# Cross attention scores from one tile per head, with the key's high and low part stacked on the partitions

## The chip, the cores and the metric

The kernel runs on one core of one Trainium2 chip. The metric is the device time of that core in microseconds. A profile is one execution of the program, recorded by the hardware. TensorE (PE) does matmuls, and its weight loads are shown apart as PEld; VectorE is called DVE, ScalarE ACT, GpSimd POOL, and SyncE (SP) issues the DMAs. The engines run their own instruction streams and wait for each other by semaphores.

## The reference

The program is a perceiver block with three stages: a cross attention, a second attention, and a mixture of experts. The change is in the first, and in its inner part:

```
q = x @ Wq                        # 8 x 128 queries, after a layernorm; 16 heads of 64
k, v = split(context @ Wkv)       # 8 x 2048 keys
sim = einsum('bhid,bhjd->bhij', q, k) * 64 ** -0.5
sim = where(mask, sim, -big)
sim = clip(sim, -5, 5)
attn = softmax(sim)
out = einsum('bhij,bhjd->bhid', attn, v)
```

Matmuls run on operands rounded to a format with a short mantissa (`F32R`). To keep float32 accuracy, the kernel splits an operand into a high part (the rounded value) and a low part (the rounded rest), and adds three products: low by high, high by low, and high by high.

## The kernel before

`stage_cross` works in slots, 64 for each of 8 batches (`SL`), so 512 in all. A slot handles 128 keys (`kt`) and four heads (`GRP`, numbered by `GL` within a half `hf` of the 16 heads). Eight slots (`BS`) share one block of 512 keys: the first four slots take the heads of `GL` 0, the other four those of `GL` 1. Each engine's body writes its order out by hand, slot by slot; the middle batches are one loop on every engine but TensorE.

TensorE in a slot s (L621 to L649):
- waits that the projection of slot s - 2 is evacuated (`p_free`) and that the scores of slot s - 2 were clipped;
- scores: for each of two pairs of heads three matmuls of 256 columns (`K_lo` by `Q_hi`, `K_hi` by `Q_lo`, `K_hi` by `Q_hi`), summed in PSUM. A pair's key is 128 partitions, 64 for each head; its query is stored with zeros, so that the left 128 columns have one head and the right 128 the other. `ps_s` has two banks, one for each of two slots in turn;
- values of slot s - 2 (`LAG`): four matmuls of 256 columns with the exponentials' high and low part side by side;
- one unit of the projection of keys or values for a later block: twelve matmuls of 512 columns into `ps_p`. The order of the units over eight slots is K, K, V, V, K, K, V, V (`IN_SLOT`), the last four for the next block. At slot 4 of 8, TensorE first waits for all four pieces of the next context block's low part (`clo_done`). The last four slots of the last batch have no projection.

ACT in slot s: the high part of the projection unit of slot s - 1 (`evac_hi`, L455), the exponential twice (L489 rounded into `E2`, L493 in full into `E`), and in slots 4 to 7 of 8 the high part of a piece of context (`C_hi`, L499). DVE: the low part of the unit (`evac_lo`, L515), the clip of `ps_s` with the mask's bound as a column (L557), and `exp_lo` of slot s - 1 (L565), the low part of the exponentials. POOL: `sums` (L427), which adds up the exponentials, and `C_lo` (L435) in slots 4 to 7 of 8.

Some slots after the last of each group of heads (four groups a batch, 32 in all) come the group's closing steps, placed by `after(s, by)`: a high and a low part of the sums, four ACT copies of 64 partitions out of `ps_o` (L477, L478), two DVE additions of 64 partitions (L529), the totals on TensorE (L609), a reciprocal (L534), a product (L541) and the store.

Lines named elsewhere: L204 and L190 are a normalization on DVE and a low part on POOL in the stage ahead; L853 and L1289 are scalings on DVE in later stages.

## Time and profile before

| | |
|---|---|
| time, median of 3 runs | 3588.77 us (3583.67 to 3590.61) |
| the profiled execution | 3591.36 us |
| its span, first to last instruction | 3589.5 us |
| PE busy | 3316.7 us (92%) |
| PEld busy | 2847.9 us (79%) |
| DVE busy | 1851.6 us (52%) |
| ACT busy | 1485.4 us (41%) |
| POOL busy | 1631.7 us (45%) |

Busy shares are means over the span. In a timeline row the first number is the start in microseconds from the span's start, the second the duration; in brackets stands how long the engine was idle before it and what ended that. A matmul's duration includes its way through the array, so that a stream of them is paced by the distance of their starts.

### The profile page before, as it was taken

What the parts mean: (1) busy time and instruction counts of PE and PEld (TensorE: products, weight loads), DVE (VectorE), ACT (ScalarE), POOL (GpSimd) and SP (SyncE); (2) the same over time, 40 slices, a digit from 0 to 9 for tenths busy, and PEclk for the clock granted to TensorE, in tenths of its full rate; (3) what the DMA queues carried; (4) which work ended last, traced back from release to release, by engine and by line L of the source; (5) the groups of instructions that cost most, each with busy time, mean ns of one, the idle gap of its engine ahead of it and who ended that gap; (6) DMA issues with size and microseconds to landing.
All of it is one profiled execution on the core that took longest, in us unless ns stands there. A gap on an engine that the chain in (4) does not pass through costs nothing. (4 is left out here: it accounts for less than half of the span.)

```text
span 3589.5 us, 52832 instructions
## 1 busy us (share of the span) xinstructions
PE 3316.7 (92%) x19140; PEld 2847.9 (79%) x19140; DVE 1851.6 (52%) x3010; ACT 1485.4 (41%) x2749; POOL 1631.7 (45%) x1122
## 2 busy tenths in 40 slices
PE   5999999999999999999999988899999586799995
PEld 4888888888888888888888876777777465578995
DVE  4454555555455555555545557566566537432213
ACT  3455555555555555555555541244344214221000
POOL 4354555555455555545545543143144035146663
PEclk9999999999999999999999989899999798899998
DMA  5211111111111011111111004100000300123220
GB/s 194 76 33 36 45 45 44 35 35 46 36 45 46 24 45 46 43 38 45 33 36 45 27 15 139 55 1 26 3 1 1 108 16 1 49 74 118 83 83 24
DMA packets 116510, 170.33 MB, mean 47 GB/s; under 512 B 12288, under 2 KB 89472, under 8 KB 107520
## 3 DMA queue, kind: packets, MB, share of 16 engines
q1 hardware_dynamic: 113408, 158.23, 14.0%
q0 software_dynamic: 2816, 8.46, 0.7%
q8 instruction: 159, 2.61, 0.3%
q14 instruction: 127, 1.04, 0.1%
HBM read 143.52 MB, written 23.13 MB: 46 GB/s over the span
## 5 line engine op out<-in xcount | busy, mean ns | idle before, releaser
L427 POOL TENSOR_TENSOR es<-es,e 128x512 f32<-128x512 f32 x480 | 622.7, 1297 | 966.7 <-ACT e L493 966.5
L489 ACT ACTIVATE e_hl<-sc 128x512 fp32r<-128x512 f32 x512 | 325.2, 635 | 739.1 <-DVE sc L557 738.8
L585 PE MATMUL ps_p<-c_hi,wkv_lo 128*128 128x512 f32 x1024 | 402.4, 393 | 4.5 <-PEq L115 4.5
L515 DVE TENSOR_TENSOR k_lo<-ps_p,k_hi 128x512 fp32r<-128x512 f32 x256 | 175.9, 687 | 438.9 <-ACT k_hi L455 438.9
L585 PE MATMUL ps_p<-c_lo,wkv_hi 128*128 128x512 f32 x1024 | 401.9, 393 | 0.0
L585 PE MATMUL ps_p<-wkv_lo,c_hi 128*128 128x512 f32 x1024 | 401.6, 392 | 0.0
L585 PE MATMUL ps_p<-wkv_hi,c_lo 128*128 128x512 f32 x1024 | 401.5, 392 | 0.0
L585 PE MATMUL ps_p<-c_hi,wkv_hi 128*128 128x512 f32 x1024 | 398.8, 389 | 0.0
L515 DVE TENSOR_TENSOR v_hl<-ps_p,v_hl 128x512 fp32r<-128x512 f32 x256 | 177.2, 692 | 428.8 <-ACT v_hl L455 427.9
L585 PE MATMUL ps_p<-wkv_hi,c_hi 128*128 128x512 f32 x1024 | 398.3, 389 | 0.0
L557 DVE TENSOR_SCALAR sc<-ps_s,topi 128x512 f32<-128x512 f32 x512 | 380.0, 742 | 0.3 <-PE ps_s L635 0.2
L565 DVE TENSOR_TENSOR e_hl<-e,e_hl 128x512 fp32r<-128x512 f32 x512 | 353.6, 691 | 0.6 <-ACT e L493 0.6
L596 PE MATMUL ps_o<-e_hl,v_hl 128*128 128x256 f32 x2048 | 330.8, 284 | 1.2 <-DVE e_hl L565 1.1
L435 POOL TENSOR_TENSOR c_lo<-raw,c_hi 128x512 fp32r<-128x512 f32 x248 | 322.2, 1299 | 0.0
L493 ACT ACTIVATE e<-sc 128x512 f32<-128x512 f32 x512 | 315.7, 617 | 0.0
L635 PE MATMUL ps_s<-q_hi,k_hi 128*128 128x256 f32 x1024 | 289.7, 283 | 0.0
L635 PE MATMUL ps_s<-q_lo,k_hi 128*128 128x256 f32 x1024 | 289.6, 283 | 0.0
L635 PE MATMUL ps_s<-q_hi,k_lo 128*128 128x256 f32 x1024 | 287.3, 281 | 0.2 <-DVE v_hl L515 0.2
L596 PEld LDWEIGHTS ps_o<-e_hl,v_hl 128*128 128x128 f32 x2048 | 283.3, 192 | 2.7 <-DVE e_hl L565 2.4
L1024 POOL TENSOR_TENSOR a_s<-a_s,a_mx 128x1536 f32<-128x1536 f32 x32 | 88.1, 2753 | 347.7 <-DVE a_mx L1107 347.7
L585 PEld LDWEIGHTS ps_p<-c_hi,wkv_hi 128*128 128x128 f32 x1024 | 192.6, 188 | 42.1
L585 PEld LDWEIGHTS ps_p<-wkv_hi,c_hi 128*128 128x128 f32 x1024 | 192.4, 188 | 42.0
(399 smaller groups left out, 7136.4 us busy)
## 6 DMA issues: line engine op xcount, KB each, us to landing
raw<-in_ctx_t SPq DMA_DIRECT2D x64, 1024.0 KB, 4.9
dense_raw<-in_L_ffn_W_experts SPq DMA_DIRECT2D x64, 256.0 KB, 3.0
raw<-in_L_xattn_Wkv SPq DMA_DIRECT2D x4, 1024.0 KB, 5.0
q_hi_scratch<-qa_qh SPq DMA_DIRECT2D x16, 256.0 KB, 2.5
q_lo_scratch<-qa_ql SPq DMA_DIRECT2D x16, 256.0 KB, 3.4
q_hi<-q_hi_scratch SPq DMA_DIRECT2D x32, 128.0 KB, 5.1
q_lo<-q_lo_scratch SPq DMA_DIRECT2D x32, 128.0 KB, 4.7
o_t_scratch<-o_sb SPq DMA_DIRECT2D x32, 128.0 KB, 2.3
```

Source lines behind the costliest of these rows:

```text
L427: g.tensor_tensor(ES[:, GL], ES[:, GL], e, ALU.add).then_inc(summed, 1)
L435: g.tensor_tensor(C_lo[:, n % 2, k, :], RAW[:, n % 2, k, :], C_hi[:, n % 2, k, :].bitcast(F32), ALU.subtract).then_inc(clo_done, 1)
L489: a.activation(E2[:, s % 2, :, 0, :], sc, ACT.Exp, scale=DH ** -0.5).then_inc(exp_hi, 1)
L493: a.activation(E[:, s % 2], SC[:, s % 2], ACT.Exp, scale=DH ** -0.5).then_inc(expd, 1)
L515: v.tensor_tensor(kv_slice(False, kind, n), ps_view(u, kind), kv_slice(True, kind, n).bitcast(F32), ALU.subtract).then_inc(p_free, 1)
L557: v.tensor_scalar(SC[:, s % 2], ps_s[:, s % 2], topi[:, kt16:kt16 + 1], -RAW_CLIP, ALU.min, ALU.max).then_inc(clipped, 1)
L565: v.tensor_tensor(E2[:, s % 2, :, 1, :], E[:, s % 2].rearrange("p (j q) -> p j q", j=GRP), E2[:, s % 2, :, 0, :].bitcast(F32), ALU.subtrac ...
L585: mm = t.matmul(ps_p[:, par % 2, :], lhs, rhs, start=m == 0, stop=m == 3 * KC - 1)
L596: mm = t.matmul(ps_o[:, 2 * GL + j // 2, (j % 2) * 256:(j % 2 + 1) * 256], V2[:, kt, GRP * GL + j, :], E2[:, s % 2, j].rearrange("p e q -> ...
L635: mm = t.matmul(ps_s[:, s % 2, pr * 256:(pr + 1) * 256], k_[:, c, kt * P:(kt + 1) * P], q_[:, hf, c, :], start=n == 0, stop=n == 2)
L1024: g_.tensor_tensor(S[:, k % 3], S[:, k % 3], each(mx[:, k % 2]), ALU.subtract).then_inc(s_shifted, 1)
```

## The change

- Scores. The key's high and low part of one head now lie on top of each other, 64 partitions each, in `K2`; the query's high and low part, each repeated on both halves of the partitions, lie side by side in `Q2`. One matmul of 256 columns for a head gives (high + low key) by high query in the left 128 columns, and by low query in the right ones. A slot has four such matmuls. They fill both banks of `ps_s`, so the next slot's scores wait until both halves are read.
- Halves. ACT copies the right halves to `RIGHT`; DVE adds them to the left ones into `SC` (`halves_added`) and clips `SC` in place, now in SBUF.
- Evacuation of a key unit takes two instructions of 64 partitions each on ACT and on DVE. On ACT it now comes behind `RIGHT`, on DVE between the addition and the clip.
- ACT's exponentials of a slot move behind the evacuation of the next slot; `exp_lo` moves from DVE to POOL, ahead of `sums`, and `C_lo` from POOL to DVE, in slots 2, 3, 6 and 7 of 8, behind the clip. `C_lo` of slots 2 and 3 is the last that TensorE waits for at slot 4.
- Values follow three slots behind (`LAG` 3); the group steps come one slot later each.
- The zeroing of Q goes, the queries' DMAs move twice the bytes.

```diff
-LAG = 2
+LAG = 3
...
-        def has_split(s, last):
-            return s % BS >= KT and not (last and s // BS + 2 >= SLB)
+        def split_at(s):
+
+            return (s // BS, s % BS - 6) if s % BS >= 6 else (s // BS - 1, s % BS)
+
+        def has_split(s, first, last):
+            return s % KT >= 2 and not (last and split_at(s)[0] + 2 >= SLB) and not (first and split_at(s)[0] < 0)
...
-                for dst, src in ((Q_hi, q_hi_d), (Q_lo, q_lo_d)):
-                    for hh in range(2):
-                        sp.dma_start(dst[hh * DH:(hh + 1) * DH, hf, :, hh * P:(hh + 1) * P].bitcast(F32),
...
+                for e, src in enumerate((q_hi_d, q_lo_d)):
+                    for r in range(2):
+                        sp.dma_start(Q2[r * DH:(r + 1) * DH, hf, :, e * P:(e + 1) * P].bitcast(F32),
...
-            for Q in (Q_hi, Q_lo):
-                g.memset(Q[:].bitcast(F32), 0.0).then_inc(zeroed, 1)
...
+            def exp_lo(i, s):
+
+                g.wait_ge(expd, i * SL + s + 1)
+                g.tensor_tensor(E2[:, s % 2, :, 1, :], E[:, s % 2].rearrange("p (j q) -> p j q", j=GRP),
+                                E2[:, s % 2, :, 0, :].bitcast(F32), ALU.subtract).then_inc(e_lo, 1)
+
             def body(i, first, last):
                 for s in range(SL):
-                    S = i * SL + s
-                    sums(i, s, first)
-                    if has_split(s, last):
-                        n, k = s // BS, s % BS - KT
-                        g.wait_ge(chi_done, KC * (i * SLB + n) + k + 1)
-                        g.tensor_tensor(C_lo[:, n % 2, k, :], RAW[:, n % 2, k, :], C_hi[:, n % 2, k, :].bitcast(F32),
-                                        ALU.subtract).then_inc(clo_done, 1)
+                    if s or not first:
+                        exp_lo(i, s - 1)
+                        sums(i, s - 1, first)
                     group_steps(i, s, first)
...
+        def evacuated(kind, n, u):
+
             out = ps_p[:, u % 2, :]
-            return out if kind == K else out.rearrange("p (h d) -> p h d", d=DH)
+            if kind == V:
+                return [(V2[:, n, :, 0:DH], V2[:, n, :, DH:], out.rearrange("p (h d) -> p h d", d=DH))]
+            return [(K2[0:DH, n, hh, :], K2[DH:, n, hh, :], out[hh * DH:(hh + 1) * DH]) for hh in range(2)]
...
+                    a.wait_ge(scored, S + 1)
+                    a.copy(RIGHT[:], ps_s[:].rearrange("p b (j e q) -> p (b j) e q", j=2, e=2)[:, :, 1, :]).then_inc(right_out, 1)
                     if s and has_kv(s - 1, last) or s == 0 and not first:
-                        evac_hi(unit_at(i, s - 1), unit_at(0, s - 1), *unit_of((s - 1) % SL)[:2])
...
+                        evac_hi(unit_at(i, s - 1), unit_at(0, s - 1), kind, n)
+                    if s or not first:
+                        exps(i, s - 1, first)
...
+                    v.wait_ge(right_out, S + 1)
+                    if not (first and s < 2):
+                        v.wait_ge(expd, S - 1)
+                    v.tensor_tensor(SC[:, s % 2].rearrange("p (j q) -> p j q", j=GRP), ps_s[:].rearrange("p b (j e q) -> p (b j) e q", j=2, e=2)[:, :, 0, :],
+                                    RIGHT[:], ALU.add).then_inc(halves_added, 1)
                     if s and has_kv(s - 1, last) or s == 0 and not first:
                         evac_lo(unit_at(i, s - 1), unit_at(0, s - 1), *unit_of((s - 1) % SL)[:2])
...
-                    v.tensor_scalar(SC[:, s % 2], ps_s[:, s % 2], topi[:, kt16:kt16 + 1], -RAW_CLIP, ALU.min, ALU.max).then_inc(clipped, 1)
-                    if s or not first:
-                        exp_lo(i, s - 1)
+                    v.wait_ge(halves_added, S + 1)
+                    v.tensor_scalar(SC[:, s % 2], SC[:, s % 2], topi[:, kt16:kt16 + 1], -RAW_CLIP, ALU.min, ALU.max).then_inc(clipped, 1)
+                    if has_split(s, first, last):
+                        n, k = split_at(s)
+                        v.wait_ge(chi_done, KC * (i * SLB + n) + k + 1)
+                        v.tensor_tensor(C_lo[:, n % 2, k, :], RAW[:, n % 2, k, :], C_hi[:, n % 2, k, :].bitcast(F32),
+                                        ALU.subtract).then_inc(clo_done, 1)
...
-                    if not (first and s < 2):
-                        t.wait_ge(clipped, S - 1)
-                    for pr in range(2):
-                        c = 2 * GL + pr
-                        for n, (k_, q_) in enumerate(((K_lo, Q_hi), (K_hi, Q_lo), (K_hi, Q_hi))):
-                            mm = t.matmul(ps_s[:, s % 2, pr * 256:(pr + 1) * 256], k_[:, c, kt * P:(kt + 1) * P],
-                                          q_[:, hf, c, :], start=n == 0, stop=n == 2)
+                    if S:
+                        t.wait_ge(halves_added, S)
+                    for j in range(GRP):
+                        mm = t.matmul(ps_s[:, j // 2, (j % 2) * 256:(j % 2 + 1) * 256], K2[:, 2 * GL + j // 2, j % 2, kt * P:(kt + 1) * P],
+                                      Q2[:, hf, GRP * GL + j, :], start=True, stop=True)
                     mm.then_inc(scored, 1)
```

## Rows read from the trace of the kernel before

**Rows 1.** Busy time by stretch, cross stage: length, engines with counts, PEclk, DMA, GB/s
```profile
111.00:2128.00 2017.00, 2016.23 (x11291) 1765.73 (x11289) 1079.90 (x1652) 1061.52 (x1922) 1023.59 (x816) 1.00 0.12 38
```

**Rows 2.** Waits of TensorE, 400 to 1800 us: total, times, longest
```profile
PE ps_o L596 <- DVE e_hl L565: 0.6, 2, 0.3
```

**Rows 3.** Timeline, TensorE, from one slot's scores to the next
```profile
1022.39 0.28 PE L635 MATMUL ps_s<-q_hi,k_lo 128*128 128x256 f32 x1
...
1023.11 0.64 PE L596 MATMUL ps_o<-e_hl,v_hl 128*128 128x256 f32 x4
...
1023.59 0.40 PE L585 MATMUL ps_p<-wkv_lo,c_hi 128*128 128x512 f32 x1
...
1026.33 0.28 PE L635 MATMUL ps_s<-q_hi,k_lo 128*128 128x256 f32 x1
```

**Rows 4.** Timeline, ACT, same slot
```profile
1022.59 0.59 ACT L455 CAST k_hi<-ps_p 128x512 fp32r<-128x512 f32 x1 [0.27 <-PE ps_p L585]
...
1024.60 0.64 ACT L489 ACTIVATE e_hl<-sc 128x512 fp32r<-128x512 f32 x1 [1.42 <-DVE sc L557]
...
1025.13 0.62 ACT L493 ACTIVATE e<-sc 128x512 f32<-128x512 f32 x1
```

**Rows 5.** Timeline, POOL and DVE, same slot
```profile
1023.14 1.30 POOL L435 TENSOR_TENSOR c_lo<-raw,c_hi 128x512 fp32r<-128x512 f32 x1
1023.21 0.69 DVE L515 TENSOR_TENSOR k_lo<-ps_p,k_hi 128x512 fp32r<-128x512 f32 x1 [1.66 <-ACT k_hi L455]
...
1023.82 0.74 DVE L557 TENSOR_SCALAR sc<-ps_s,topi 128x512 f32<-128x512 f32 x1
...
1025.83 1.29 POOL L427 TENSOR_TENSOR es<-es,e 128x512 f32<-128x512 f32 x1 [1.39 <-ACT e L493]
```

**Rows 6.** Timeline, group steps on 64 partitions
```profile
1009.91 0.37 ACT L478 COPY t<-ps_o 64x256 f32<-64x256 f32 x1
1010.31 0.37 ACT L477 COPY t<-ps_o 64x256 f32<-64x256 f32 x1
...
1011.10 0.86 DVE L529 TENSOR_TENSOR u<-ps_o,t 64x256 f32<-64x256 f32 x2 [2.06 <-ACT t L478]
```

**Rows 7.** One line's instructions: duration ns min/median/max, first and last start
```profile
L853 DVE TENSOR_SCALAR t_s<-t_s x1: 419/419/419, 2246.8 to 2246.8; 128x512 f32<-128x512 f32 x1
```
```profile
L1289 DVE TENSOR_SCALAR rows<-p_x,p_mom,p_rs x8: 539/546/548, 2821.4 to 2848.7; 128x512 f32<-128x512 f32 x8
```

**Rows 8.** Timeline, scores released by an evacuation, near the stage's end
```profile
2127.41 0.69 DVE L515 TENSOR_TENSOR v_hl<-ps_p,v_hl 128x512 fp32r<-128x512 f32 x1 [1.99 <-ACT v_hl L455]
...
2128.16 0.38 PE L635 MATMUL ps_s<-q_hi,k_lo 128*128 128x256 f32 x1 [0.21 <-DVE v_hl L515]
2128.38 0.28 PE L635 MATMUL ps_s<-q_lo,k_hi 128*128 128x256 f32 x1
```

**Rows 9.** L204 and L190 in the window 17.0 to 17.5 us
```profile
L204 DVE TENSOR_SCALAR qa_x<-qa_x,qa_mom,qa_rs x2: 4712/4730/4748, 12.8 to 17.4; 128x512 f32<-128x512 f32 x2
```
```profile
L190 POOL TENSOR_TENSOR qa_wq_lo<-raw,qa_wq_hi x2: 4529/4606/4682, 12.7 to 17.2; 128x2048 fp32r<-128x2048 f32 x2
```

**Rows 10.** DVE and POOL at the stage's end: timeline, L427's first instruction there
```profile
2129.98 0.69 DVE L565 TENSOR_TENSOR e_hl<-e,e_hl 128x512 fp32r<-128x512 f32 x1
...
2131.57 0.80 DVE L565 TENSOR_TENSOR e_hl<-e,e_hl 128x512 fp32r<-128x512 f32 x1
...
2139.85 1.26 POOL L409 TENSOR_TENSOR es_lo<-es,es_hi 128x512 fp32r<-128x512 f32 x1
...
2139.90 1.50 DVE L541 TENSOR_TENSOR o_sb<-u,rec 128x256 f32<-128x256 f32 x1 [0.24 <-DVE rec L534]
```
```profile
L427 POOL TENSOR_TENSOR es<-es,e x1: 1797/1797/1797, 2130.0 to 2130.0; 128x512 f32<-128x512 f32 x1
```

**Rows 11.** Groups by form: count, busy us, mean ns, idle before
```profile
L565 DVE TENSOR_TENSOR e_hl<-e,e_hl 128x512 fp32r<-128x512 f32 x512 | 353.6, 691 | 0.6 <-ACT e L493 0.6
...
L534 DVE RECIPROCAL rec<-ps_o 128x256 f32<-128x256 f32 x32 | 55.9, 1746 | 1.4 <-PE ps_o L609 1.4
```

More of the change, by code:

```diff
@@ L386, in body @@
                         queries(i + 1, 0)
-                    for n in after(s, 6):
+                    for n in after(s, 7):
                         if n >= 0 or not first:
@@ L454, in evac_hi @@
                 a.wait_ge(proj_done, u + 1)
-                a.copy(kv_slice(True, kind, n), ps_view(par, kind)).then_inc(kv_hi, 1)
+                for hi, lo, src in evacuated(kind, n, par):
+                    ins = a.copy(hi, src)
+                ins.then_inc(kv_hi, 1)
             for u, (kind, n) in enumerate(AHEAD):
@@ L461, in group_steps @@
                 s %= SL
-                for n in after(s, 2):
+                for n in after(s, 3):
                     if n >= 0 or not first:
@@ L468, in group_steps @@
                         a.copy(ES_hi[:], ES[:, n % 2]).then_inc(es_hi, 1)
-                for n in after(s, 3):
+                for n in after(s, 4):
                     if n >= 0 or not first:
@@ L478, in group_steps, with exps @@
                             a.copy(T2[hh * DH:(hh + 1) * DH], o4[DH:P, :, hh, 0, :]).then_inc(o_copied, 1)
+            def exps(i, s, first):
+                S = i * SL + s
+                a.wait_ge(clipped, S + 1)
+                if not (first and s < 2):
+                    a.wait_ge(pv_done, S - 1)
+                sc = SC[:, s % 2].rearrange("p (j q) -> p j q", j=GRP)
+                a.activation(E2[:, s % 2, :, 0, :], sc, ACT.Exp, scale=DH ** -0.5).then_inc(exp_hi, 1)
+                if not (first and s < 2):
+                    a.wait_ge(e_lo, S - 1)
+                    a.wait_ge(summed, S - 1)
+                a.activation(E[:, s % 2], SC[:, s % 2], ACT.Exp, scale=DH ** -0.5).then_inc(expd, 1)
             def body(i, first, last):
@@ L502, in _ @@
             for s in TAIL:
+                if s == SL:
+                    exps(B, -1, False)
                 group_steps(B, s, False)
@@ L521, in group_steps @@
                 s %= SL
-                for n in after(s, 3):
+                for n in after(s, 4):
                     if n >= 0 or not first:
@@ L530, in group_steps @@
                                             ).then_inc(o_read, 1)
-                for n in after(s, 5):
+                for n in after(s, 6):
                     if n >= 0 or not first:
@@ L534, in group_steps @@
                         v.reciprocal(flat(REC[:]), ps_o[:, 2 * (n % 2), 0:2 * P]).then_inc(rec_done, 1)
-                for n in after(s, 6):
+                for n in after(s, 7):
                     if n >= 0 or not first:
@@ L646, in body @@
                         project(kind, n, of, cb, unit_at(i, s))
-                    for n in after(s, 4):
+                    for n in after(s, 5):
                         if n >= 0 or not first:
@@ L654, in _ @@
                 values(s, B - 1, SL * (B - 1) + s, False)
[L655 removed]
+            for n in (-2, -1):
+                total(B, n)
 G4 = 4
```

64 lines of the change are left out of this document (23 added, 41 removed).

## The prediction

> **What bounds the kernel now.** I read the page first: TensorE is busy for 92% of the span, as the table above has it, and every other engine for about half. The view by stretches shows where: in the cross attention stage, from 111 to 2128 us, TensorE has 2016.23 of 2017 us at the full clock (2.4 GHz), and DVE, ACT and POOL about half of that [rows 1]. The waits agree: from 400 to 1800 us TensorE waited 0.6 us, twice, for anything [rows 2]. So the stage lasts as long as TensorE's stream. The timeline gives its parts: scores start at 1022.39, values at 1023.11, projection at 1023.59, the next scores at 1026.33. A slot is 3.94 us: six score matmuls at 0.12, four value matmuls at 0.12, twelve projection matmuls in 2.74 [rows 3]. The last four slots have no projection, so 508 slots last 3.94 us (508 x 3.94 + 31 totals of 0.48 = 2016).
>
> **What the change takes off TensorE.** Four score matmuls in place of six, so a slot's stream is 3.70 us, and 508 x 0.24 = 122 us could go. Whether they go depends on what TensorE now waits for before scores: `halves_added` of the slot before, and `p_free` of the projection two slots back. Both are now behind longer work. I lay out one slot, with 0 at its first score matmul.
>
> **Prices.** ACT: an exp takes 0.64 or 0.62, and the next instruction follows 0.54 after its start (0.50 after a copy from PSUM, my estimate with the same overlap of 0.09); a cast from PSUM takes 0.59; from the end of ACT's cast to DVE's start pass 0.03, from an exp to POOL 0.07 to 0.08 [rows 4, 5]. DVE: PSUM minus SBUF 0.69, the next 0.61 after it; two SBUF inputs 0.69 [rows 5, 11]. POOL: 1.30. Instructions on 64 partitions do not overlap with what follows: copies of 0.37 come 0.39 apart, two DVE ones take 0.86 together, 0.43 each [rows 6]. So each half of a split key evacuation costs 0.61 on ACT and 0.72 on DVE. `RIGHT` and the adding are not in the trace; nearest are the 0.59 cast and the 0.69 subtraction with one PSUM and one SBUF input. The clip now reads SBUF: between 0.42 (no column operand) and 0.55 (two) [rows 7] against 0.74 from PSUM [rows 5]; with one column I take 0.48. A late `p_free` costs 0.16: DVE ended at 2128.10, the matmul came at 2128.16, its successor 0.22 later instead of 0.12 [rows 8].
>
> **The slot without any contention.** The last score matmul ends at 0.36 + 0.28 = 0.64. ACT copies `RIGHT` 0.67 to 1.26; DVE adds 1.29 to 1.98, so `halves_added` has 1.7 us in hand. Value slots: ACT's evacuation 1.16 to 1.75, DVE's 1.90 to 2.59, in time. Key slots (half of all): ACT halves at 1.16 and 1.77, done 2.36; DVE halves at 2.39 and 3.11, done 3.80; next scores at 3.80 + 0.16 = 3.96. So a key slot is 3.96, no shorter than before, and only value slots fall to 3.70. ACT has room: its longest slot, key and split, is done at 3.96, and the next `RIGHT` comes at 4.63. Without contention the sum is 254 x 0.24 - 254 x 0.02 = 56 us less.
>
> **DVE against POOL.** POOL now does `exp_lo` and `sums` back to back (2.6 us of each slot), and DVE gets two instructions that read SBUF alone: the clip, and `C_lo` in every second slot. The trace shows that such instructions exclude each other. Two `L204` instructions, of the form that takes 0.55 us alone, took 4.75 and 4.71 beside two POOL instructions of 4.53 and 4.68: one got through between the two of POOL, the other had to wait out the second [rows 7, 9]. At 2139.85 POOL began 0.05 before a DVE instruction of 0.42, which then took 1.50 and ended 0.29 after POOL's; at 2129.98 DVE began 0.05 earlier, and POOL's 1.30 became 1.80, ending 1.16 after DVE's [rows 10]. A subtraction of 512 ended 0.54 after POOL's (2131.57 + 0.80 against 2130.03 + 1.80). So: who starts first holds the port; the waiting side gets it next, then the other; a blocked clip ends 0.3 and a blocked subtraction 0.55 after POOL, and POOL 1.15 after DVE. DVE with one PSUM input isn't touched: `k_lo` took 0.69 at 1023.21 beside `c_lo` on POOL at 1023.14 [rows 5]. Before, the two hardly met: `L565`, with two SBUF inputs, had a mean of 0.69 [rows 11]. In a key slot ACT's exps end at 3.54, so `exp_lo` starts at 3.61, ahead of the clip, asked for at 3.83.
>
> I follow four slots from the start of the first key slot (us):
> - **Key, no split (0).** `exp_lo` 3.61 to 4.90; clip done 5.20; `sums` done 6.35.
> - **Key, split (3.96).** DVE adds at 5.25, evacuates until 7.76; `exp_lo` 7.57 to 8.86; clip done 9.16; `sums`, already waiting, gets the port until 10.31; `C_lo` done 10.86.
> - **Value, split (7.92).** DVE is free at 10.78 instead of 9.2: adding until 11.47, evacuation until 12.08, so `p_free` sets the next slot at 12.24, not 11.62. The clip and `C_lo` stand behind `exp_lo` (until 12.0) and `sums` (13.6): `C_lo` done 14.15.
> - **Value, no split (12.24).** Adding from 14.07, evacuation until 15.37, in time; the next slot at 15.94.
>
> That is 15.94 for 4 x 3.94 = 15.76: the whole saving is gone, and 0.18 more. And in every second group of four TensorE wants all four pieces of `C_lo` at 12.24 + 0.96 = 13.20 to project from the next block; the last comes at 14.15. That is 0.95, with 0.1 for the restart 1.05. Eight slots: 2 x 0.18 + 1.05 = 1.41 us more. There are 64 blocks of eight; the first and the last lack splits or projections: 62 x 1.41 = 87 us.
>
> By the Trainium skill (SBUF — State Buffer, "SBUF: two separate sides") the shared port pair is an exclusive lock held for the full instruction, and the loser fully blocks. The order is the one of the rows; but by the page a blocked clip or subtraction would end its full 0.48 or 0.68 after POOL, 0.3 later in each four slots, 38 us more in all. The rows show 0.3 and 0.55, so I keep those.
>
> **Smaller terms.** The reciprocal (1.75 us on DVE [rows 11]) now falls in a key slot whose DVE is free only at 5.12: the next adding starts at 6.87 instead of 5.25, keys are done at 8.81, the next slot comes 1.05 late. The value slot behind it gives back 0.6 of that, its evacuation being late anyway; where the slot after it waits for `C_lo` nearly all of it stays. I take 0.7 for each of 32 groups: 22 us, from 0 (the delay falls in waits that are there anyway) to 56 (1.75 each). The 64-partition copies and totals fall in value slots with room. Batch starts put the `topi` copy and its loop entry on a DVE that is late: some 0.7 us x 7 = 5. The last four slots now run at POOL's 2.6 us or at the loop scores, `RIGHT`, adding (2.0), against about 1.5: with the third slot of lag 6 us. Queries move twice the bytes, 1 MB for each half batch, a half batch ahead of use on DMA engines that are 12% busy: nothing; uncovered, at 38 / 0.12 = 317 GB/s [rows 1], each of 16 loads would cost 3.3. The zeroing of Q (two memsets before the first query DMA) goes, but scores found their queries without a wait: nothing.
>
> **Sum:** 87 + 22 + 5 + 6 = 120 us. The profiled execution lasted 3591.36 us (span 3589.5), 2.6 above the median of 3588.77; 3589 + 120 = **3709 us**.
>
> **Rivals.**
> - *`C_lo` gets the port before `sums`* (or the clip needs no port). This ends faster. It decides at 9.16 in the second slot: if DVE keeps the port when its next instruction stands ready, `C_lo` is done at about 9.7, the adding of the third slot starts at 9.75, its evacuation ends at 11.05 and the slot is 3.70. Then four slots take 15.32, TensorE waits some 0.2 to 0.5 for the last `C_lo`: eight slots save 0.4 to 0.7 us, 62 x 0.55 = 34, less 10 for groups and tail: 3565. For it: the DVE instruction is only 0.08 from its predecessor's end. Against: in [rows 9] exactly such a follower had to wait 4.71 for POOL's second instruction. Chance 0.16.
> - *DVE and POOL don't hurt, the key chain alone binds or not even that*: 3589 - 56 + 8 = 3541 if 64-partition instructions don't overlap, 3467 if they do and TensorE stays the bound. For it: means in the trace before are undisturbed; against: those means come from a phase in which the engines happened to take turns. Chance 0.07.
> - *It cancels*: the shifts hit slots that have room and 122 us are eaten almost exactly, within 7 us of 3589. Chance 0.07.
> - *It gets worse*: `exp_lo` with its strided views is slower on POOL than 1.30, or a TensorE wait of a microsecond, of which this stretch has none, costs clock; half a microsecond more in each four slots is 62 us, 3775. For it: nothing is left in hand; against: after a wait of 0.21 us the matmuls were back at 0.28 [rows 8]. Chance 0.10.
>
> **How the numbers follow.** Forecast 0.60, with its own range of 3640 to 3755 (groups 0 to 56; `C_lo` partly hidden takes off 30). The range for 8 in 10 reaches down to the first rival's 3545 and up to 3765; outside are the unhindered cases and the worst. Faster: 0.16 + 0.07 = 0.23. Same, within 0.2% (7 us, about what this kernel's runs can tell): 0.07. Slower: 0.70.
>
> **What would show it.** Right: the clip's mean near 1.2 us instead of 0.48; `C_lo` on DVE well over 1; POOL's two at 1.3 to 1.5; DVE busy most of the stage; TensorE idle for about a tenth of it, before scores for the evacuation and once in eight slots before the projection for `c_lo`; score matmuls still 0.12 apart, slots of 4.1 us on average. Wrong: clip at 0.5, slots of 3.7 and 3.96 in turn, TensorE's wait for `c_lo` absent. The prediction fails if the port is granted in another order, since one instruction's place decides 100 us.

## The result

The changed kernel takes 3703.4 us (median of 4 runs, 3697.57 to 3712.39) against 3589.69 us (4 runs, 3583.67 to 3592.53) on the same chip: a ratio of 1.0321, 95% interval 1.0302 to 1.0341. It is slower by 114 us; 3709 was forecast. The profiled execution has a span of 3710.5 us, 121.0 more than the 3589.5 of before. It is the slowest of the four runs, 9 us over their median, so the sums below, made on the profiled spans, explain 121 us and not 114.

The page of the changed kernel first, its engines and the groups that matter (busy us, mean ns of one, idle time before them):

```profile
PE 3297.8 (89%) x18116; PEld 2700.9 (73%) x18116; DVE 2610.7 (70%) x3514; ACT 1839.8 (50%) x3517; POOL 2051.7 (55%) x1384
...
L432 POOL TENSOR_TENSOR e_hl<-e,e_hl 128x512 fp32r<-128x512 f32 x512 | 659.2, 1287 | 704.2 <-ACT e L497 704.2
L428 POOL TENSOR_TENSOR es<-es,e 128x512 f32<-128x512 f32 x480 | 705.8, 1470 | 0.0
...
L581 DVE TENSOR_SCALAR sc<-sc,topi 128x512 f32<-128x512 f32 x512 | 549.4, 1073 | 8.2
L576 DVE TENSOR_TENSOR sc<-ps_s,right 128x512 f32<-128x512 f32 x512 | 350.8, 685 | 182.7 <-ACT right L503 176.6
...
L585 DVE TENSOR_TENSOR c_lo<-raw,c_hi 128x512 fp32r<-128x512 f32 x248 | 408.5, 1647 | 0.0
```

The clip (L581) has a mean of 1.07 us and `C_lo` (L585) one of 1.65. Both read SBUF alone. The adding (L576), which has one operand in PSUM, has 0.69, as the PSUM subtraction had before.

The same stretch as [rows 2], waits from 400 to 1800 us (total, times, longest). PE are TensorE's matmuls; PEld are its weight loads, which can wait while a matmul still runs:

```profile
PEld ps_s L652 <- DVE k_hl L536: 86.0, 167, 1.5
PEld ps_s L652 <- DVE v_hl L536: 59.9, 78, 1.8
...
PEld ps_p L605 <- DVE c_lo L585: 49.1, 41, 1.6
PE ps_p L605 <- DVE c_lo L585: 40.7, 41, 1.4
PE ps_s L652 <- DVE v_hl L536: 29.1, 67, 1.6
PE ps_s L652 <- DVE k_hl L536: 22.5, 21, 1.1
```

Before, TensorE waited 0.6 us in this stretch. Now it waits for DVE in three places: the evacuation of keys, that of values, and, 41 times, `C_lo`. The three PE rows add up to 92.3 us, which is what TensorE's busy time (1307.7) leaves of these 1400. The stretch that answers to [rows 1]:

```profile
111.00:2240.00 2129.00, 1993.97 (x10271) 1617.21 (x10270) 1843.60 (x2154) 1412.59 (x2682) 1438.78 (x1073) 1.00 0.13 40
```

TensorE's clock is still at its full level. DVE's busy time in the stage rose from 1080 to 1844 us, but part of that is blocked time.

The timeline of TensorE, starts of the scores of eight slots (and of the one projection that waits), answers to [rows 3]:

```profile
970.16 0.64 PE L652 MATMUL ps_s<-q_hl,k_hl 128*128 128x256 f32 x4
...
973.97 0.74 PE L652 MATMUL ps_s<-q_hl,k_hl 128*128 128x256 f32 x4
...
977.89 0.74 PE L652 MATMUL ps_s<-q_hl,k_hl 128*128 128x256 f32 x4
...
982.19 0.74 PE L652 MATMUL ps_s<-q_hl,k_hl 128*128 128x256 f32 x4 [0.33 <-DVE v_hl L536]
...
986.00 0.64 PE L652 MATMUL ps_s<-q_hl,k_hl 128*128 128x256 f32 x4
...
998.02 0.74 PE L652 MATMUL ps_s<-q_hl,k_hl 128*128 128x256 f32 x4 [0.34 <-DVE v_hl L536]
...
1000.11 0.50 PE L605 MATMUL ps_p<-c_hi,wkv_lo 128*128 128x512 f32 x1 [0.87 <-DVE c_lo L585]
1002.97 0.64 PE L652 MATMUL ps_s<-q_hl,k_hl 128*128 128x256 f32 x4
```

From 970.16 to 1002.97 eight slots take 32.81 us; before they took 8 x 3.94 = 31.52, and 32.93 was forecast. The last slot, from 998.02, is the one of 4.95 in which the projection waits for `C_lo`.

POOL and DVE in the first three of these slots, which answer to [rows 5]:

```profile
977.54 1.29 POOL L432 TENSOR_TENSOR e_hl<-e,e_hl 128x512 fp32r<-128x512 f32 x1 [1.19 <-ACT e L497]
978.78 1.48 POOL L428 TENSOR_TENSOR es<-es,e 128x512 f32<-128x512 f32 x1
980.94 1.28 POOL L432 TENSOR_TENSOR e_hl<-e,e_hl 128x512 fp32r<-128x512 f32 x1 [0.67 <-ACT e L497]
982.18 1.50 POOL L428 TENSOR_TENSOR es<-es,e 128x512 f32<-128x512 f32 x1
```

```profile
971.45 0.69 DVE L576 TENSOR_TENSOR sc<-ps_s,right 128x512 f32<-128x512 f32 x1 [1.68 <-ACT right L503]
972.52 1.39 DVE L536 TENSOR_TENSOR k_hl<-ps_p,k_hl 64x512 fp32r<-64x512 f32 x2 [0.38 <-ACT k_hl L460]
...
977.87 1.24 DVE L581 TENSOR_SCALAR sc<-sc,topi 128x512 f32<-128x512 f32 x1
979.03 1.79 DVE L585 TENSOR_TENSOR c_lo<-raw,c_hi 128x512 fp32r<-128x512 f32 x1
980.85 0.69 DVE L576 TENSOR_TENSOR sc<-ps_s,right 128x512 f32<-128x512 f32 x1
981.46 0.68 DVE L536 TENSOR_TENSOR v_hl<-ps_p,v_hl 128x512 fp32r<-128x512 f32 x1
982.05 0.47 DVE L581 TENSOR_SCALAR sc<-sc,topi 128x512 f32<-128x512 f32 x1
982.45 1.78 DVE L585 TENSOR_TENSOR c_lo<-raw,c_hi 128x512 fp32r<-128x512 f32 x1
```

Lay the two over each other. The clip of 977.87 comes when POOL's `exp_lo` has run for 0.33 us; `exp_lo` ends at 978.83, the clip at 979.11. `C_lo` follows at 979.03, but `sums` has the port since 978.78; it ends at 980.26, `C_lo` at 980.82, and only then can DVE add the scores of the next slot (980.85). Its evacuation ends at 982.14 and releases the scores of 982.19. Where POOL's instruction is about to end, the same clip takes 0.47 (982.05).

### The profile page after: what moved, and what is told of

Read it like the earlier page. It is cut to its first block and busy times, and to the rows that moved or that the text cites. A ratio compares the mean times of both kernels' runs of the same rounds, so it can differ in the third digit from the quotient of the medians.

```text
span 3710.5 us, 52342 instructions
## 1 busy us (share of the span) xinstructions
PE 3297.8 (89%) x18116; PEld 2700.9 (73%) x18116; DVE 2610.7 (70%) x3514; ACT 1839.8 (50%) x3517; POOL 2051.7 (55%) x1384
## 5 line engine op out<-in xcount | busy, mean ns | idle before, releaser
L432 POOL TENSOR_TENSOR e_hl<-e,e_hl 128x512 fp32r<-128x512 f32 x512 | 659.2, 1287 | 704.2 <-ACT e L497 704.2
L503 ACT COPY right<-ps_s 128x512 f32<-128x512 f32 x512 | 300.7, 587 | 712.6 <-PE ps_s L652 712.3
L581 DVE TENSOR_SCALAR sc<-sc,topi 128x512 f32<-128x512 f32 x512 | 549.4, 1073 | 8.2
L576 DVE TENSOR_TENSOR sc<-ps_s,right 128x512 f32<-128x512 f32 x512 | 350.8, 685 | 182.7 <-ACT right L503 176.6
L652 PEld LDWEIGHTS ps_s<-q_hl,k_hl 128*128 128x128 f32 x2048 | 282.3, 189 | 229.5 <-DVE k_hl L536 129.5
L652 PE MATMUL ps_s<-q_hl,k_hl 128*128 128x256 f32 x2048 | 364.9, 300 | 77.0 <-DVE v_hl L536 42.1
L536 DVE TENSOR_TENSOR k_hl<-ps_p,k_hl 64x512 fp32r<-64x512 f32 x512 | 352.7, 689 | 95.8 <-ACT k_hl L460 91.3
L585 DVE TENSOR_TENSOR c_lo<-raw,c_hi 128x512 fp32r<-128x512 f32 x248 | 408.5, 1647 | 0.0
L460 ACT CAST k_hl<-ps_p 64x512 fp32r<-64x512 f32 x512 | 298.4, 583 | 13.9 <-PE ps_p L605 10.9
L605 PEld LDWEIGHTS ps_p<-c_hi,wkv_lo 128*128 128x128 f32 x1024 | 193.5, 189 | 112.4 <-DVE c_lo L585 74.2
```

What stands on the lines that cost most here:

```text
L432: g.tensor_tensor(E2[:, s % 2, :, 1, :], E[:, s % 2].rearrange("p (j q) -> p j q", j=GRP), E2[:, s % 2, :, 0, :].bitcast(F32), ALU.subtrac ...
L503: a.copy(RIGHT[:], ps_s[:].rearrange("p b (j e q) -> p (b j) e q", j=2, e=2)[:, :, 1, :]).then_inc(right_out, 1)
L536: ins = v.tensor_tensor(lo, src, hi.bitcast(F32), ALU.subtract)
L576: v.tensor_tensor(SC[:, s % 2].rearrange("p (j q) -> p j q", j=GRP), ps_s[:].rearrange("p b (j e q) -> p (b j) e q", j=2, e=2)[:, :, 0, :] ...
L581: v.tensor_scalar(SC[:, s % 2], SC[:, s % 2], topi[:, kt16:kt16 + 1], -RAW_CLIP, ALU.min, ALU.max).then_inc(clipped, 1)
L585: v.tensor_tensor(C_lo[:, n % 2, k, :], RAW[:, n % 2, k, :], C_hi[:, n % 2, k, :].bitcast(F32), ALU.subtract).then_inc(clo_done, 1)
```

## The experiments

The table has them all. "Scores" is the time from the first to the last start of a score matmul, read from the view of that line; it leaves out what happens in other stages. Before's time is the median of its runs on the same chip, which differed by up to 0.3% between chips. A ratio without an interval is one run against that median. From the last score to the end these runs take 1446 us (experiment 3) to 1476 us (10), though nothing is changed there: a single time can be off by some 15 us, and the scores are the surer measure.

| kernel | time, us | before, us | ratio | scores, us |
|---|---|---|---|---|
| before | 3589.69 | | | 2022.1 |
| changed | 3703.4 | 3589.69 | 1.0321 (1.0302 to 1.0341) | 2136.3 |
| 1 `C_lo` before `sums` | 3617.34 | 3588.76 | 1.0087 (1.0069 to 1.0105) | 2045.8 |
| 2 no `C_lo` | 3569.74 | 3588.76 | 0.9947 | 2001.7 |
| 3 no adding | 3556.56 | 3588.76 | 0.9910 | 2002.4 |
| 4 neither | 3524.96 | 3588.76 | 0.9822 | 1959.1 |
| 5 neither, whole keys | 3493.08 | 3599.75 | 0.9704 | 1919.0 |
| 6 keys first | 3649.7 | 3599.75 | 1.0139 | 2065.8 |
| 7 keys first, `C_lo` before `sums` | 3548.31 | 3599.75 | 0.9871 (0.9847 to 0.9896) | 1974.6 |
| 8 exchange undone | 3687.86 | 3592.85 | 1.0264 | 2114.8 |
| 9 as 7, `topi` later | 3542.74 | 3592.85 | 0.9862 (0.9840 to 0.9885) | 1967.4 |
| 10 `topi` later alone | 3722.59 | 3599.75 | 1.0341 | 2131.9 |
| 11 exchange in the kernel before | 3651.01 | 3592.85 | 1.0163 (1.0140 to 1.0185) | 2078.9 |

The starts of the score matmuls also give the length of every slot. The eight that repeat where no group or batch ends (medians, us; the fifth is the one whose projection needs all of the next block's `C_lo`):

| kernel | eight slots | sum |
|---|---|---|
| before | 3.94 each | 31.52 |
| changed | 3.80 3.81 3.92 4.30 4.94 3.81 3.92 4.30 | 32.80 |
| 1 | 3.70 3.81 3.92 3.80 4.35 3.81 3.92 3.80 | 31.11 |
| 4 | 3.70 3.81 3.91 3.80 3.70 3.81 3.91 3.80 | 30.44 |
| 5 | 3.70 each | 29.60 |
| 6 | 3.81 3.70 3.75 3.90 5.16 3.70 3.75 3.90 | 31.67 |
| 7 | 3.70 3.70 3.75 3.70 4.12 3.70 3.75 3.70 | 30.12 |
| 8 | 3.80 3.81 4.02 4.19 4.43 3.81 4.02 4.19 | 32.27 |

### 1. One wait more on POOL

```diff
                         exp_lo(i, s - 1)
+                        if has_split(s, first, last):
+                            g.wait_ge(clo_done, KC * (i * SLB + split_at(s)[0]) + split_at(s)[1] + 1)
                         sums(i, s - 1, first)
```

> The changed kernel, with one wait more: in the slots that split a part of the context, POOL starts its running sum only when DVE's C_lo of this slot is done. No work is added or left out. Theory (port order: C_lo loses its place in the shared port to POOL's second instruction, ends over a microsecond late, and the next slot's adding with it): C_lo falls back from a mean of 1.65 us to 1.0 or less, the slot after it from 4.94 to about 4.0, eight slots from 32.80 to about 31.0 us, and the time to 3585 us, plus or minus 25. Rival one (the sheer amount of DVE's work bounds): the amount is the same, so 3690 to 3710. Rival two (POOL is nearly as full as DVE, and its sums, held back, delay the second exponential of ACT): C_lo is short, but the time stays above 3680.

This kernel has the same instructions as the changed one and one more wait, and it is 2.3% faster. The rival of the amount of DVE's work is refuted, and so is that of POOL's fullness. DVE and POOL in its timeline, the slots that answer to 977.54 and 980.94 above:

```profile
681.60 1.28 POOL L432 TENSOR_TENSOR e_hl<-e,e_hl 128x512 fp32r<-128x512 f32 x1 [1.19 <-ACT e L499]
683.84 1.31 POOL L428 TENSOR_TENSOR es<-es,e 128x512 f32<-128x512 f32 x1 [0.96 <-DVE c_lo L587]
685.10 1.52 POOL L432 TENSOR_TENSOR e_hl<-e,e_hl 128x512 fp32r<-128x512 f32 x1
```

```profile
681.93 1.24 DVE L583 TENSOR_SCALAR sc<-sc,topi 128x512 f32<-128x512 f32 x1
683.09 0.68 DVE L587 TENSOR_TENSOR c_lo<-raw,c_hi 128x512 fp32r<-128x512 f32 x1
683.80 0.69 DVE L578 TENSOR_TENSOR sc<-ps_s,right 128x512 f32<-128x512 f32 x1
...
685.46 1.72 DVE L587 TENSOR_TENSOR c_lo<-raw,c_hi 128x512 fp32r<-128x512 f32 x1
```

`C_lo` at 683.09 takes 0.68 in the place of 1.79. The second one, at 685.46, still stands behind `exp_lo`, which has run since 685.10; that is the 4.35 us slot that is left, and why the mean of `C_lo` is 1.16 from 400 to 1800 us and not 1.0 or less. The eight slots came out at 31.11 for an expected 31.0, but the whole missed its range by 7 us: outside the eight, a batch costs 9.6 us (258.5 less 8 x 31.11) where it costs 7.2 in the changed kernel (269.6 less 8 x 32.80). Experiment 9 comes back to that.

### 2 to 4. Without `C_lo`, without the adding, without both

Experiment 2, on ACT and on DVE:

```diff
-                        a.copy(C_hi[:, n % 2, k, :], RAW[:, n % 2, k, :]).then_inc(chi_done, 1)
+                        a.copy(C_hi[:, n % 2, k, :], RAW[:, n % 2, k, :]).then_inc(clo_done, 1)
...
-                        v.wait_ge(chi_done, KC * (i * SLB + n) + k + 1)
-                        v.tensor_tensor(C_lo[:, n % 2, k, :], RAW[:, n % 2, k, :], C_hi[:, n % 2, k, :].bitcast(F32),
-                                        ALU.subtract).then_inc(clo_done, 1)
```

Experiment 3, on DVE (ACT's exponentials wait for `halves_added` in the place of `clipped`); 4 is both:

```diff
-                    v.tensor_tensor(SC[:, s % 2].rearrange("p (j q) -> p j q", j=GRP), ps_s[:].rearrange("p b (j e q) -> p (b j) e q", j=2, e=2)[:, :, 0, :],
-                                    RIGHT[:], ALU.add).then_inc(halves_added, 1)
+                    v.tensor_scalar(SC[:, s % 2].rearrange("p (j q) -> p j q", j=GRP), ps_s[:].rearrange("p b (j e q) -> p (b j) e q", j=2, e=2)[:, :, 0, :],
+                                    topi[:, kt16:kt16 + 1], -RAW_CLIP, ALU.min, ALU.max).then_inc(halves_added, 1)
...
-                    v.wait_ge(halves_added, S + 1)
-                    v.tensor_scalar(SC[:, s % 2], SC[:, s % 2], topi[:, kt16:kt16 + 1], -RAW_CLIP, ALU.min, ALU.max).then_inc(clipped, 1)
```

> The changed kernel without DVE's 248 subtractions of C_lo (the low part of the context is left out: it keeps what the first loads put there; TensorE's waits go by ACT's copy of the high part). Theory (the one long stall in four slots is C_lo's): the 4.94 us slot is gone, the four slots keep the key chain's 3.9 and the clip's blocked start, about 3550 us (3535 to 3575). Rival (amount of DVE's work: 1.65 x 248 = 409 us of its 2610 busy, so 2200): DVE is no longer near full, so the amount says the same here; it differs in the run that leaves the adding out. Rival (the reciprocal's groups and the batch ends hold the loss): no less than 3650.

> The changed kernel without the adding of the two halves: DVE clips the left half straight from PSUM, in one instruction in the place of two, and the scores' right half is left out (ACT still copies it). C_lo stays on DVE, and the two instructions on POOL stay. Theory (the clip of two SBUF tiles is the one that waits for the port behind POOL's exp_lo; read from PSUM it does not, so C_lo comes to its place earlier, beside exp_lo and not beside the sums): the clip 0.5 to 0.7 us, about 3550 us (3535 to 3590). Rival (C_lo is stalled by POOL wherever it comes, since two instructions stand back to back there): C_lo still takes 1.6 us or more, and the time is 3600 to 3670.

> The changed kernel without the adding and without C_lo (the scores' right half and the context's low part are left out as in the two runs before it): no instruction of DVE in the common slot works on two SBUF operands. Theory: what is left is the key slot's chain, RIGHT, two halves on ACT and two on DVE before the next projection, and the groups: key slots 3.9, value slots 3.7, eight slots 30.4 us, 3535 to 3555 us. Rival (score tiles of half the depth, written once and freed by the adding alone, hold TensorE themselves): 3600 or more with all of DVE's port traffic gone.

Without `C_lo` the scores take 134.6 us less, without the adding and the SBUF clip 133.9, without both 177.2. The two don't add up: the eight slots are 30.4 us without `C_lo`, 30.7 without the adding and 30.4 without both, so taking away either gives back nearly the whole loss there, as in one chain of blocked instructions. Experiment 3 shows it directly. `C_lo` is the same instruction as in the changed kernel, and no wait or order was set for it (duration min/median/max, ns):

```profile
L583 DVE TENSOR_TENSOR c_lo<-raw,c_hi x248: 680/1372/1387, 132.2 to 2068.9; 128x512 fp32r<-128x512 f32 x124
```

```profile
L585 DVE TENSOR_TENSOR c_lo<-raw,c_hi x248: 677/1781/1793, 138.9 to 2209.0; 128x512 fp32r<-128x512 f32 x124
```

The first is experiment 3, the second the changed kernel: 1.37 in the place of 1.78 at the median. It is still blocked, but nothing on DVE is blocked ahead of it, so it comes beside `exp_lo` and not beside `sums`: one that starts at 903.44 ends at 904.81, 0.54 after the `exp_lo` that ran from 902.98. The clip from PSUM has a mean of 0.75, the 0.74 of before. With both gone (4), the eight slots are 30.44, the key chain alone, as forecast (30.4). The time, 3524.96, is 10 us under its range all the same: a batch costs 2.6 us outside the eight slots (246.1 less 8 x 30.44), where it costs 2.2 before and 7.2 in the changed kernel, so the extra cost of groups and batch starts goes with these two instructions as well.

### 5. Whole keys

```diff
-            return [(K2[0:DH, n, hh, :], K2[DH:, n, hh, :], out[hh * DH:(hh + 1) * DH]) for hh in range(2)]
+            return [(K2[:, n, 0, :], K2[:, n, 1, :], out)]
```

> The run without the adding and without C_lo, and with the key projection evacuated in one instruction of 128 partitions on ACT and one on DVE, in the place of two of 64 each (the scores' right half and the context's low part are left out, and the key's two parts are laid out so that the scores mean nothing; the amount of TensorE's work is that of the changed kernel). Theory (of the key slots' 3.8 and 3.9 us, what is over TensorE's own 3.70 is the evacuation in halves): all eight slots 3.70, 29.6 us, and 3524 less 64 x 0.85, about 3475 us (3460 to 3500). Rival (the 0.1 us in the key slots is TensorE's own, say of the score matmuls' reading the two new tiles): no change from 3525.

All slots are 3.70 us, TensorE's own stream; the 0.84 us in eight slots was the evacuation in halves. The time is in its range, 18 us over the 3475 in its middle, on a chip on which before took 0.3% more; by ratios 4 and 5 differ by 1.2%, 42 us, for 52 (62 x 0.84). The rest went at the batch starts (see 9).

### 6 and 7. The order on ACT and DVE in key slots

On ACT in 6; on DVE the same is done with `evac_lo`, ahead of the adding. 7 is this and the edit of 1.

```diff
+                    keys = (s and has_kv(s - 1, last) or s == 0 and not first) and unit_of((s - 1) % SL)[0] == K
+                    if keys:
+                        evac_hi(unit_at(i, s - 1), unit_at(0, s - 1), *unit_of((s - 1) % SL)[:2])
                     a.wait_ge(scored, S + 1)
...
-                    if s and has_kv(s - 1, last) or s == 0 and not first:
+                    if (s and has_kv(s - 1, last) or s == 0 and not first) and not keys:
```

> The changed kernel with another order in the slots that follow a key projection: ACT evacuates the key's high halves before it copies the scores' right half, DVE the low halves before it adds. Nothing is left out. Theory: p_free no longer hangs on the score, so 3.81 and 3.92 become 3.70 to 3.75 where nothing else is late, and the adding that follows a stalled C_lo costs less; but C_lo still loses the port to POOL's second instruction, so the greater part of the loss stays: 3640 to 3690 us. Rival (the key chain is what makes C_lo late): the loss is gone, 3600 or less. Rival (the adding, now last, frees the one score tile later): 3720 or more.

> The changed kernel with both orders: keys evacuated first, and POOL's running sum after C_lo in the slots that split. Nothing is left out. Theory: from the 3617 us of the one order alone, eight slots from 31.10 to 30.0 to 30.4, which is 45 to 70 us, so 3545 to 3575 us, under the kernel before. Rival (C_lo of the second of the two splitting slots, which stands behind POOL's exp_lo, still holds the projection): the slot of 4.35 stays and only 0.1 to 0.2 us is won in each of six others, 3575 to 3600.

Experiment 6 is in its range: the key slots fall to 3.70 and 3.75, the slot with the late `C_lo` rises from 4.94 to 5.16, and the projection there waits 1.07 us for it, for 0.87 in the changed kernel.

With both orders (7) the scores take 161.7 us less than in the changed kernel, and 90.5 + 70.5 = 161 is the sum of the two alone. The kernel leaves nothing out and is faster than before by 1.3% (0.9847 to 0.9896). The slot whose projection needs `C_lo` fell to 4.12, against the rival by which it stays at 4.35. So 161.7 us of the changed kernel's scores, more than the 114.2 that it lost against before, hang on the order of work that is all there in both.

### 8 and 11. The exchange of `exp_lo` and `C_lo` alone

Experiment 11 makes the exchange in the kernel before, first on POOL, then on DVE behind the clip; 8 undoes it in the changed kernel in the same way.

```diff
+                    exp_lo(i, s)
                     sums(i, s, first)
-                    if has_split(s, last):
-                        n, k = s // BS, s % BS - KT
-                        g.wait_ge(chi_done, KC * (i * SLB + n) + k + 1)
-                        g.tensor_tensor(C_lo[:, n % 2, k, :], RAW[:, n % 2, k, :], C_hi[:, n % 2, k, :].bitcast(F32),
-                                        ALU.subtract).then_inc(clo_done, 1)
...
-                    if s or not first:
-                        exp_lo(i, s - 1)
+                    if has_split(s, last):
+                        n, k = s // BS, s % BS - KT
+                        v.wait_ge(chi_done, KC * (i * SLB + n) + k + 1)
+                        v.tensor_tensor(C_lo[:, n % 2, k, :], RAW[:, n % 2, k, :], C_hi[:, n % 2, k, :].bitcast(F32),
+                                        ALU.subtract).then_inc(clo_done, 1)
```

> The changed kernel with one part undone: exp_lo, in every slot, back on DVE (behind the clip), and C_lo, in every second slot, back on POOL (behind the running sum). Nothing is left out. Theory (what costs is an instruction on two SBUF tiles on DVE that comes while POOL has two in a row): the long slot of 4.9 us goes, since C_lo is no longer on DVE, but now exp_lo waits for POOL's in all slots and DVE's four instructions fill them: 3.9 to 4.1 us for each slot, 3610 to 3670 us. Rival (exchanging the two was the whole loss): at or under 3550, what the kernel without C_lo had plus little. Rival (DVE's sheer amount): 512 instructions in the place of 248, each 0.69, so slower than 3700.

> The kernel before with one part of the change alone: exp_lo on POOL (ahead of the running sum), C_lo on DVE (behind the clip). No adding, no stacked keys, values two slots behind. Theory (the exchange costs where DVE has no idle time left, and the kernel before has some 1 to 2 us in a slot; its clip reads PSUM and is not held by POOL): C_lo takes 1.2 to 1.8 us on DVE, yet the time moves by less than 0.8%, 3590 to 3620 us. Rival (a late C_lo is late for the projection in any kernel): slower by 2% and more, 3660 and up. Rival (POOL's 1.3 us in the place of DVE's 0.7 makes e_lo late for the values two slots behind): slower by 1 to 2%, with TensorE's waits at the value matmuls.

Undoing the exchange gives back 21.5 of the 114.2 us. The slots are at the expected 4.03 on average (32.27 / 8), but the time is above the range, since outside the eight a batch now costs 8.7 us (266.9 less 8 x 32.27). DVE is busy for 1322 of the 1400 us from 400 to 1800. Its `exp_lo` has a mean of 1.18 and its clip one of 1.04, so blocking is there too. The rival by which the amount of work decides, slower than 3700, did not come, but this one run is only 12 us under it; experiment 1 speaks against it more clearly.

In the kernel before, the exchange costs 56.8 us of scores, for under 30 expected: a miss. The time, 1.6% over before, is what the third rival gave, but its sign is absent: in the whole stage TensorE waited twice for `exp_lo` at a value matmul, 2.0 us together. For `C_lo` it never waited ahead of a projection, as the second rival had it. The ordinary slots stay at 3.94, with `C_lo` at 1.38; the loss is around the ends of groups and of batches, in slots of 5.0 to 5.7 and some of 4.4. One of them on DVE:

```profile
649.27 1.53 DVE L563 TENSOR_TENSOR c_lo<-raw,c_hi 128x512 fp32r<-128x512 f32 x1 [1.73 <-ACT c_hi L501]
650.72 1.75 DVE L536 RECIPROCAL rec<-ps_o 128x256 f32<-128x256 f32 x1
652.38 0.62 DVE L517 TENSOR_TENSOR k_lo<-ps_p,k_hi 128x512 fp32r<-128x512 f32 x1
...
655.39 1.38 DVE L563 TENSOR_TENSOR c_lo<-raw,c_hi 128x512 fp32r<-128x512 f32 x1 [1.73 <-ACT c_hi L501]
656.69 1.50 DVE L543 TENSOR_TENSOR o_sb<-u,rec 128x256 f32<-128x256 f32 x1
658.11 0.68 DVE L517 TENSOR_TENSOR k_lo<-ps_p,k_hi 128x512 fp32r<-128x512 f32 x1
```

`C_lo` waits for ACT and then for `exp_lo`; the reciprocal, and in the next slot a multiplication of 0.42 that takes 1.50 behind `sums`, stand between it and the key's evacuation, and the scores of 658.84 wait 1.55 us for `k_lo`. My expectation had counted the idle time of the ordinary slot and left out that of the group slots.

### 9 and 10. The start of a batch

```diff
-                    if s == 0:
-                        if not first:
-                            v.wait_ge(clipped, S)
-                        v.tensor_copy(topi[:], top[:, bass.ds(i * (M // P), M // P)]).then_inc(topi_done, 1)
-                        v.wait_ge(topi_done, i + 1)
                     kt16 = place(s)[1] * KT + s % KT
...
+                    if s == 0:
+                        if not first:
+                            v.wait_ge(clipped, S)
+                        v.tensor_copy(topi[:], top[:, bass.ds(i * (M // P), M // P)]).then_inc(topi_done, 1)
+                        v.wait_ge(topi_done, i + 1)
                     v.wait_ge(halves_added, S + 1)
```

> The changed kernel with DVE's copy of the batch's clip bounds (topi, 8 in the run) moved behind the adding and the evacuation of the batch's first slot. Nothing is left out. Theory (the adding that frees the one score tile waits behind topi, which before stood only ahead of a clip with a second tile behind it): the copy's 0.8 us and its 0.2 of wait leave the path, 8 to 16 us in 8 batches, 3688 to 3697. Rival (the time ahead of it, in which DVE only issues, is the cost, and it stays wherever the copy stands): 3700 to 3706.

> The run with both orders (keys evacuated first, POOL's sum after C_lo), and the copy of the batch's clip bounds moved behind the adding and the evacuation of the batch's first slot. Nothing is left out. Theory (the first two slots of each batch after the first, 6.65 and up to 5.36 us, are TensorE waiting about 2 us for p_free and halves_added behind that copy, after which its granted clock is low for some us): the wait falls by 1 us, the clock stays up, 3548 less 7 x 1.0 to 7 x 3.5, so 3520 to 3542 us. Rival (the time in which the engines only issue at the batch's start is the wait, and the clock falls all the same): 3543 to 3555.

The start of a batch in 7, DVE, then TensorE's next scores, then stretches of 2 us:

```profile
603.74 0.68 DVE L575 COPY topi<-top 128x16 f32 x1 [2.41 <-issue]
604.62 0.69 DVE L584 TENSOR_TENSOR sc<-ps_s,right 128x512 f32<-128x512 f32 x1 [0.21 <-DVE topi L575]
605.23 0.68 DVE L541 TENSOR_TENSOR v_hl<-ps_p,v_hl 128x512 fp32r<-128x512 f32 x1
```

```profile
605.96 0.84 PE L660 MATMUL ps_s<-q_hl,k_hl 128*128 128x256 f32 x4 [2.03 <-DVE v_hl L541]
```

```profile
603.30:605.30 2.00, 0.64 (x4) 0.43 (x4) 1.35 (x3) 1.07 (x2) 2.00 (x2) 1.00 0.02 4
605.30:607.30 2.00, 1.34 (x8) 1.34 (x9) 1.96 (x4) 0.46 (x1) 0.99 (x2) 0.79 0.02 4
607.30:609.30 2.00, 2.00 (x7) 1.61 (x7) 1.93 (x4) 1.28 (x3) 0.38 (x1) 0.50 0.00 0
609.30:611.30 2.00, 2.00 (x9) 1.65 (x8) 1.61 (x1) 0.00 (x0) 2.00 (x2) 0.86 0.00 0
```

TensorE waited 2.03 us, and then its granted clock (the number after the counts) was 0.79, 0.50 and 0.86: the lower of the two levels, 1.2 GHz, for some 3 us. This batch's first two slots are 6.65 and 5.36 us. The same batch in 9, scores and the stretch behind them:

```profile
605.72 0.74 PE L660 MATMUL ps_s<-q_hl,k_hl 128*128 128x256 f32 x4 [1.01 <-DVE v_hl L541]
```

```profile
606.10:608.10 2.00, 2.00 (x14) 1.78 (x13) 1.93 (x3) 1.20 (x3) 0.99 (x2) 1.00 0.01 4
```

The wait is 1.01 and the clock stays up; the first two slots are 5.63 and 3.95 us. That is the expected effect in place, but the third slot gives some of it back (4.58 us, for 3.7 to 4.2 in most batches of 7), and the scores fall by 7.2 us only. DVE's idle time at this place did not go either: 2.2 to 2.5 us of it now stand ahead of the adding. The time is 3542.74, between the 3520 to 3542 of the theory and the 3543 to 3555 of the rival, and the intervals of 7 and 9 overlap: in the time of the whole kernel the move is worth nothing that these runs can tell. Alone (10) it took the first slot from 6.03 to between 5.1 and 5.3 us and 4.4 us off the scores; the single time lies above both expectations, with the other stages longer in that run, and decides nothing.

## Why the prediction was right

**The key chain.** Forecast 3.96 for both key slots; 3.81 and 3.92 measured. The steps are there: the adding starts 1.29 after the scores, the first key half 2.36, both are done 3.75 after them (971.45, 972.52 and 973.91, with the scores at 970.16 and 973.97). The step that was too dear is the restart: 0.06 from DVE's end to the first matmul and 0.10 more for its successor, as [rows 8] show, but the second belongs to the following slot, where it delays `RIGHT` and makes the next key slot 3.92. Experiment 4 has this chain alone, 30.44 for eight slots, where the forecast's case without contention would have had 4 x 3.96 + 4 x 3.70 = 30.64. Experiment 5 shows that the halves are its whole cost.

**The order at the port.** This carried the forecast. Experiments 1 and 7 confirm it by moving nothing but order, and experiment 3 by taking the clip of SBUF away ahead of an unchanged `C_lo`. In the common slot a blocked clip ends 0.28 after POOL's instruction (979.11 and 978.83), forecast 0.3; a blocked `C_lo` 0.56 after (980.82 and 980.26), forecast 0.55. The clip's forecast mean was near 1.2 and is 1.07, since in one of four slots, as at 982.05, it passes at the end of `exp_lo` and ahead of `sums` and takes 0.47. `exp_lo` starts 3.57 after the scores (forecast 3.61), the clip is asked for at 3.90 (3.83). The third slot is 4.30 (4.32), the wait for `C_lo` adds 1.14 (1.05). The rival by which DVE keeps the port when its next instruction stands ready needed `C_lo` done soon after the clip; it is done 1.71 after it (979.11 to 980.82), and that rival's 3565 is nearly what experiment 2 gives without `C_lo` altogether. Experiment 1 forces that rival's order: the eight slots then save 0.41 us, as it said (0.4 to 0.7), but the kernel takes 3617, since the groups and batch starts cost more than the 10 us that it had for them and the tail.

By the Trainium skill (SBUF — State Buffer, "SBUF: two separate sides") the loser fully blocks. The trace agrees in the order, a blocked instruction always ends after the winner, but a clip of 0.48 ends 0.28 and not 0.48 after POOL, and a subtraction of 0.68 ends 0.56 after it. The forecast took the rows' 0.3 and 0.55, and those held.

**The sum.** Eight slots cost 32.80 less 31.52, 1.28 for a forecast 1.41; times 62 that is 79.4 for 87. A batch's first two slots cost 1.5 more than elsewhere (9.94 less 8.11 for slots 32 and 33 of a batch, in the changed kernel, less 0.3 of the same before) in five of the seven batches; in the second and the last, whose first slots are 4.78 and 4.60 and not 6.03, it is 0.6 and 0.4. Together that is 8.4 for 5. Scores grew by 114.2; of that 2.2 are the last three slots, so 24.2 remain for the groups: 22 forecast. The last three slots and what follows the last score cost 2.2 + 3.2 = 5.4 for 6. The first scores come 1.7 later, which was not forecast, and 1.9 lie in other stages. Together 79.4 + 8.4 + 24.2 + 5.4 + 1.7 + 1.9 = 121.0 us, by which the spans differ. The group term is a remainder here, but the starts show it too: slots 32 to 63 of a batch hold the steps of two groups and grew by 1.66 to 1.75 more than four times 1.28, 0.86 for each group where 0.7 was forecast. The mechanism is the forecast's: the key slot that holds the reciprocal takes 5.03 for 3.92 (1.11 late, forecast 1.05), and the slot behind it gives back 0.50 (forecast 0.6). The eight slots came out 8 us under their term, the batch starts, the groups and what was not forecast 9 us over theirs: that 120 meets 121 so closely is luck.

**What the forecast's signs said.** TensorE waits for evacuations and, 41 times in 1400 us, for `c_lo`; the slots are 4.1 on average (32.80 / 8); POOL's two are at 1.29 and 1.47. TensorE's idle share in the row from 111 to 2240 us is 6%, where a tenth was forecast: the slots did grow by a tenth over 3.70, but a matmul's busy time reaches past its stream's end, and short gaps vanish in it.

**What it did not see.** That 161.7 us hang on two orders which cost nothing. The forecast held the loss to be the price of the change; it is the price of DVE's `C_lo` meeting the second of POOL's two instructions, and of adding ahead of the keys.

What stays open: the split of the 24 us for groups into reciprocal and multiplication was not tried alone, though the key slot that holds the reciprocal is 5.03 us in experiments 1 and 2 and 3.91 in 3, where the clip ahead of it is not blocked. Open, too, is DVE's idle time ahead of `topi` ("issue"). It is there only in the five batches that DVE enters by its loop's jump back: 0.96 to 1.27 us before, 0.91 to 1.06 in the changed kernel, 2.25 to 2.51 in experiment 7. In the second batch and the last it is 0.03 or nothing. What sets its length no run here shows.

## What to carry to other kernels

Where two engines exclude each other on SBUF, price each instruction by what it stands behind, not by its mean: lay four slots side by side and ask which of the two is already waiting when the port comes free. Then set that order by a wait, and put the step that another engine waits for (here the key's evacuation) ahead of the one that has slack (the adding); the same instructions were worth 162 us more in another order. An idle share in the ordinary slot says nothing of the slots that carry a group's or a batch's extra steps, where the same exchange cost 57 us.
